# Adding the two states of a scan step on TensorE instead of GpSimd, with a refitted table of places

## The chip, the cores and the metric

The kernel runs on one core of one Trainium2 chip. The metric is the device time in microseconds of one launch. A core has five engines that work side by side and wait for each other by semaphores: TensorE (PE, with PEld for its weight loads), VectorE (DVE), ScalarE (ACT), GpSimd (POOL) and SyncE (SP), which here only issues DMAs. Everything is float32 except a few operands of the attention.

## What is computed

The input x (32 sequences of 256 positions with 256 channels) goes through four layers: a Mamba block on a permutation of the positions, softmax attention with 16 heads, a second Mamba block, and linear attention. The core of a Mamba block is a recurrence over the 256 positions for each of 512 channels and 16 states:

```python
def step(hst, inp):
    dt_t, B_t, C_t, x_t = inp
    dA = jnp.exp(dt_t[:, :, None] * A)
    hst = hst * dA + (dt_t * x_t)[:, :, None] * B_t[:, None, :]
    y = jnp.einsum('bds,bs->bd', hst, C_t)
    return (hst, y)
...
y = jnp.transpose(ys, (1, 0, 2)) + xm * D_param
y = y * jax.nn.silu(z)
return y @ W_out
```

The change is about the einsum: for every channel the 16 states, each multiplied by its row of C, are added up.

## The kernel before, in words

Two sequences are one group of T = 512 columns, and there are 16 groups. In each group each of the two Mamba blocks has one scan: the 512 channels are four chunks of 128 partitions, the 16 states are taken in pairs, and so a scan has 32 steps (STEPS, eight for each chunk, PER). There are 16 groups x 2 blocks x 32 = 1024 steps in all. A step handles two states of one chunk, side by side in a tile of 128 x 2 x 512:

- SyncE loads two rows of B into `bs` and two rows of C into `cs`, each spread over all partitions, 512 KB each (`scan_sync`, L1024). Each ring has two tiles. B's load of a step waits for the product (L952) two steps earlier, C's load for the multiplication by C (L984) two steps earlier, and both stand in one queue, in this order.
- ScalarE makes the decays `da` (L902), two instructions.
- VectorE multiplies dt*x, which lies in PSUM, by `bs` (L952) and runs the recurrence over the positions (L966), whose result is the tile `hw` of a ring of four (RING).
- GpSimd multiplies `hw` by `cs` (`times_c`, L984) and then adds the two halves of the tile (`add_pair`, L991).
- TensorE adds the 128 x 512 sum to the PSUM bank `yps` with a matmul by the identity (`reduce`, L853). The eight steps of a chunk accumulate there, started by the skip term (L868). Then VectorE multiplies the bank by silu(z) into `dtx` (`gated`, L935). The recurrence of a step may write its tile of the ring only when the matmul of four steps earlier is done.

Around the scans runs the rest of the network, the side work, on the same engines: the front of a Mamba block (layer norm, input projection, convolution of four taps on VectorE at L796, step sizes), its rest (z, the second half of the step sizes), its back (output projection L1056; in block 0 a gather of positions by one-hot matrices, L1066; gate and residual, L1094 and L1102), the attention of each sequence (scores and their maxima, L1207 and L1347; exponentials, L1313; product with V, L1251), and linear attention. While block 0 scans one group, block 1 scans the one before it, in turn, and the side work of neighbouring groups is laid among both.

Each engine has one queue. Its order is fixed by numbers: `PLACES` says for each piece of side work and each engine behind which part of which scan step an operation stands (5.442 is in step 5, behind 0.442 of it), and `AT` says where in a step the scan's own operations stand (the recurrence at 0.33, `reduce` at 0.3 with the tile of two steps earlier, the addition at 0.55). `iteration` merges the scan and two lanes of side work by these numbers. The middle groups run in a loop (`Fori`), the first and last ones are written out.

Of the kernel before, what the change touches and what calls it, by code (L numbers as in the profile page):

```python
# [192 lines left out]
AT = {"reduce": 0.3, "restart": 0.5, "decay": 0.1, "scan": 0.33, "times_c": 0.05, "add": 0.55, "load": 0.2, "chunk": 0.5}  # L193
# [10 lines left out]
        "pe": [-1.5, 0.8, 3.967, 6.633, 9.845, 10.391, 13.55],  # L204
        "act": [0.033, 0.067, 5.3, 5.9, 8.433, 9.433, 12.475, 12.6],
        "dve": [10.498, 10.832, 13.165, 14.11, 14.22],
        "pool": [11.3, 14.8, 15.3],
# [3 lines left out]
        "pe": [27.467, 27.633, 27.8, 27.967, 28.133, 28.55, 28.8, 29.05, 30.467, 30.633, 30.8, 31.133],  # L211
        "act": [24.35, 26.35, 26.6, 26.85, 28.211, 28.322, 28.433, 28.544, 28.656, 28.767, 28.878, 29.35, 29.6,
               29.85],
        "dve": [26.165, 26.247, 29.382, 29.433, 29.485, 29.536, 29.588, 29.639, 29.691, 29.742, 29.794, 29.845,
               29.897, 29.948, 30.553, 31.082, 31.165, 31.247],
        "pool": [26.8, 31.8, 32.05, 32.3],
# [3 lines left out]
        "pe": [24.8, 25.05, 25.54, 25.78, 26.02, 28.8, 30.55, 30.675, 30.8, 30.925, 31.175, 32.05],  # L220
        "act": [23.98, 24.6, 25.225, 25.35, 25.725, 25.85, 25.975, 29.331, 29.408, 29.485, 29.638, 29.792,
               29.869, 30.023],
        "dve": [23.665, 24.165, 26.665, 27.665, 28.11, 28.22, 28.665, 29.11, 29.22, 29.404, 29.553, 29.628,
               29.777, 29.926, 30.665, 31.497, 31.663, 31.83],
        "pool": [24.3, 31.8, 32.05, 32.3],
        "sp": [30.533, 30.867],
    },
    "back0": {
        "pe": [1.9, 3.467, 3.633, 3.8, 4.133],
        "act": [0.6, 4.433, 4.767, 5.5],  # L230
        "dve": [5.442, 5.553, 5.665, 5.777, 5.888],
        "pool": [-1.5, 2.3],
# [3 lines left out]
        "pe": [14.967, 17.7, 18.1],  # L236
        "act": [14.767, 20.9],
        "dve": [16.165, 16.665, 18.665, 19.165, 20.665],
        "pool": [20.717, 21.3],
# [7 lines left out]
        "act": [5.7, 6.6, 7.3, 8.211, 8.322, 8.544, 8.656, 8.767, 8.878, 8.989, 9.767, 11.433, 11.767, 12.225,  # L247
               12.35, 12.725, 12.85, 12.975, 14.433, 14.767, 15.3, 15.65, 15.725, 15.8, 15.875, 18.243, 18.386,
               18.529, 18.671, 18.814, 19.386, 19.529, 19.671, 19.814, 19.957, 20.3, 22.6, 23.7, 23.9],
        "dve": [6.11, 6.22, 8.665, 9.165, 10.414, 10.581, 10.665, 10.749, 10.916, 11.082, 11.165, 11.248,  # L250
               11.665, 16.553, 16.777, 17.165, 17.442, 17.553, 17.665, 17.777, 17.888, 18.165, 22.066, 22.132,
               22.198, 22.264, 24.665, 26.082],
        "pool": [6.8, 22.8, 24.217],
# [7 lines left out]
        "act": [0.025, 0.05, 0.075, 0.433, 0.767, 1.6, 3.267, 3.433, 3.6, 3.767, 8.267, 8.433, 8.6, 8.767,  # L261
               8.933, 9.211, 9.322, 9.433, 9.544, 9.656, 9.767, 9.989, 11.35, 11.6, 11.85, 15.3, 16.3, 16.5,
               16.7, 16.9, 17.267, 17.433, 17.6, 17.767, 17.933, 18.6, 20.3, 20.5, 20.7],
        "dve": [-1.5, -0.5, 2.665, 3.165, 4.665, 5.165, 5.665, 6.165, 6.665, 7.498, 7.665, 7.832, 8.165, 13.165,
               13.553, 13.777, 14.11, 14.22, 14.665, 15.11, 15.22, 15.553, 19.553, 19.777, 20.11, 20.22,
               22.553, 22.777],
        "pool": [0.275, 20.883, 21.8],
# [3 lines left out]
        "pe": [23.55, 24.05, 24.55, 26.26, 28.55, 29.05, 29.8, 30.425, 31.05, 31.55, 31.8],  # L271
        "act": [23.62, 23.74, 23.86, 25.475, 25.6, 26.433, 26.767, 29.177, 29.254, 29.562, 29.715, 29.946],
        "dve": [21.665, 22.165, 24.665, 25.165, 25.665, 26.11, 26.22, 26.497, 26.832, 27.165, 29.479, 29.702,
               29.851, 31.997, 32.163],
        "pool": [22.8, 30.217, 30.383],
# [3 lines left out]
        "pe": [17.05, 17.78, 18.729, 19.8, 20.133, 21.8, 22.467, 22.633, 25.7, 26.1, 30.967],  # L279
        "act": [15.575, 15.95, 16.025, 18.957, 19.243, 20.5, 20.7, 20.9, 21.6, 24.6, 24.85, 28.989],  # L280
        "dve": [15.165, 15.665, 18.665, 19.165, 19.497, 19.665, 19.832, 20.165, 20.665, 21.165, 23.165, 23.665,
               24.165, 28.665, 30.777],
        "pool": [16.3, 24.383, 27.8],
# [1569 lines left out]
```

## Time and profile before

| what | value |
|---|---|
| median of 3 runs | 5616.87 us |
| lowest and highest run | 5615.27 and 5630.38 us |
| profiled execution, its own time | 5616.71 us |
| span of its trace | 5614.9 us |
| VectorE busy | 4895.1 us (87%) |
| TensorE busy | 4463.3 us (79%) |
| GpSimd busy | 4077.3 us (73%) |
| ScalarE busy | 3463.0 us (62%) |

The span goes from the first to the last instruction of one execution. Busy is the time in which an engine had at least one instruction under way. A float32 matmul instruction appears as two records. Matmuls are pipelined, so the next one starts before the one ahead has ended, and a run of matmuls counts one such end as busy. PEclk is the granted TensorE clock as a share of the full one.

### The profile page before, as it was taken

How to read it: one execution, taken by the hardware profiler on the slowest of the kernel's cores; microseconds unless marked ns; L12 is line 12 of the kernel's file. 1: busy time of each engine (PE TensorE's matmuls, PEld its weight loads, DVE VectorE, ACT ScalarE, POOL GpSimd, SP SyncE). 2: the span in 40 equal slices, each digit the busy share in tenths (PEclk: the TensorE clock that was granted, in tenths of full speed). 3: DMA queues.
4: the chain of work that ended last, by engine and by line, in shares of the span. 5: the costliest groups of instructions: out<-in, count | busy, mean ns of one | idle time of the engine just before them, and what ended most of it. 6: DMA issues, size and time to landing. Idle time of an engine off the chain costs nothing.

```text
span 5614.9 us, 66460 instructions
## 1 busy us (share of the span) xinstructions
PE 4463.3 (79%) x15736; PEld 2300.2 (41%) x15736; DVE 4895.1 (87%) x5146; ACT 3463.0 (62%) x6182; POOL 4077.3 (73%) x2847
## 2 busy tenths in 40 slices
PE   4577888888788878888888888888788888888755
PEld 1233344444444434444444444444444444444323
DVE  3749999999999999999999999999999999999482
ACT  2346666667666666766666666766666676766352
POOL 2728787877878877777877777777877777787272
PEclk8678899999999999999999999999999899998775
DMA  4516666666667666666666666666666666666161
GB/s 143 193 64 232 213 231 214 225 219 207 233 202 228 225 219 221 212 229 201 224 225 221 218 219 224 207 227 212 222 212 223 219 210 228 214 228 209 63 209 51
DMA packets 350275, 1147.58 MB, mean 204 GB/s; under 512 B 38790, under 2 KB 79275, under 8 KB 349835
## 3 DMA queue, kind: packets, MB, share of 16 engines
q1 hardware_dynamic: 305674, 1088.05, 58.7%
q10 hardware_dynamic: 44160, 54.60, 3.1%
q8 instruction: 161, 2.64, 0.2%
q14 instruction: 280, 2.29, 0.1%
HBM read 1123.47 MB, written 19.04 MB: 203 GB/s over the span
## 4 chain that ended last, share of the span: by engine, by line
POOL 41%; issue 26%; DVE 12%; PE 10%; DMA 5%; ACT 4%; POOLq 1%; SPq 1%; DVEq 0%; ACTq 0%
POOL hw L984 30%; POOL hw L991 8%; DVE hw L966 5%; DMA cs<-bc_scratch 3%; DVE ps L952 3%; DMA bs<-bc_scratch 2%; PE ps L1139 1%; POOL rstd L611 1%; POOL dtx L840 1%; DVE u L796 1%; PE ps L853 1%; PE ps L677 1%; PE ps L1056 1%; PE ps L1148 1%; PE ps L1131 1%
## 5 line engine op out<-in xcount | busy, mean ns | idle before, releaser
L984 POOL TENSOR_TENSOR hw<-hw,cs 128x1024 f32<-128x1024 f32 x1024 | 2419.6, 2363 | 887.9 <-DVE hw L966 824.6
L966 DVE TENSOR_TENSOR_SCAN hw<-da,ps 128x1024 f32<-128x1024 f32 x1024 | 2334.2, 2279 | 59.7 <-ACT da L902 20.0
L902 ACT ACTIVATE da<-dt,a_neg 128x510 f32<-128x510 f32 x2048 | 1331.3, 714 | 359.9 <-DVE hw L966 357.8
L952 DVE TENSOR_TENSOR ps<-ps,bs 128x1024 f32<-128x1024 f32 x1024 | 1254.5, 1225 | 138.2 <-DMA bs<-bc_scratch 85.5
L991 POOL TENSOR_TENSOR hw<-hw 128x512 f32<-128x512 f32 x1024 | 1301.2, 1271 | 70.8
L853 PE MATMUL ps<-hw,ident 128*128 128x512 f32 x2048 | 1139.3, 663 | 129.1 <-POOL hw L991 128.8
L672 PE MATMUL ps<-hT,w_in 128*128 128x512 f32 x1024 | 532.6, 656 | 209.2 <-ACT sz L774 117.8
L853 PEld LDWEIGHTS ps<-hw,ident 128*128 128x128 f32 x2048 | 389.0, 208 | 571.3 <-issue 293.3
L1313 ACT ACTIVATE pts<-ps,mcur 128x256 f32<-128x256 f32 x1024 | 401.0, 476 | 251.6 <-PE ps L1236 249.8
L549 ACT ACT_TABLE_LOAD x353 | 452.9, 1283 | 54.7 <-issue 48.6
L1347 DVE TENSOR_REDUCE mx<-ps 128x2 f32<-128x512 f32 x512 | 330.0, 678 | 81.8 <-PE ps L1207 80.9
L672 PEld LDWEIGHTS ps<-hT,w_in 128*128 128x128 f32 x1024 | 190.2, 200 | 482.1 <-issue 231.4
L1200 PE MATMUL ps<-mb,pick 128*128 128x512 f32 x512 | 261.6, 547 | 127.5 <-DVE mx L1347 88.2
L1229 PE MATMUL ps<-nm,pick 128*128 128x512 f32 x512 | 243.7, 532 | 100.7 <-DVE nm L1352 66.2
L796 DVE SCALAR_TENSOR_TENSOR u<-ps,cols,u 128x510 f32<-128x510 f32 (+2 forms) x384 | 274.7, 735 | 34.2 <-ACT u L720 29.3
L1251 PE MATMUL ps<-pts,va 128*32 128x256 f32 x2048 | 276.2, 396 | 24.1 <-ACT pts L1313 22.5
L1056 PE MATMUL ps<-w_out,dtx 128*128 128x256 f32 x1024 | 249.2, 399 | 28.2 <-DVE dtx L935 26.5
L840 POOL TENSOR_TENSOR dtx<-dt,u 128x512 f32<-128x512 f32 x128 | 161.4, 1272 | 131.1 <-DVE dt L816 131.1
L1131 PE MATMUL ps<-rows,ones 1*128 1x512 f32 x320 | 188.9, 671 | 63.9 <-DVE xhat_b L1523 32.5
L1056 PEld LDWEIGHTS ps<-w_out,dtx 128*128 128x128 f32 x1024 | 199.9, 199 | 93.4 <-DVE dtx L935 34.5
L606 POOL TENSOR_TENSOR rstd<-mv,eps 128x2 f32<-128x2 f32 (+1 forms) x96 | 19.1, 199 | 279.6 <-DVE mv L601 277.8
L1200 PEld LDWEIGHTS ps<-mb,pick 128*128 128x128 f32 x512 | 96.0, 199 | 294.8 <-DVE mx L1347 206.6
(186 smaller groups left out, 5994.1 us busy)
## 6 DMA issues: line engine op xcount, KB each, us to landing
bs<-bc_scratch SPq DMA_DIRECT2D x1024, 512.0 KB, 5.0
cs<-bc_scratch SPq DMA_DIRECT2D x1024, 512.0 KB, 4.1
xhat<-in_x ACTq DMA_DIRECT2D x16, 512.0 KB, 4.4
gate<-gates_scratch ACTq DMA_DIRECT2D x64, 128.0 KB, 4.7
x_b<-in_x ACTq DMA_DIRECT2D x16, 512.0 KB, 7.3
x_scratch<-x_b ACTq DMA_DIRECT2D x16, 512.0 KB, 2.9
x_c<-x_scratch ACTq DMA_DIRECT2D x16, 512.0 KB, 5.5
out<-x_c ACTq DMA_DIRECT2D x32, 256.0 KB, 2.5
```

The costliest lines, as they stand in the source:

```text
L549: nc.scalar.preload_act_table_set(name)
L672: ins = nc.tensor.matmul(side[pc.bank[f"m{m}"]], w_in[l][:, k, m * P:(m + 1) * P], hT[:, k, :], start=(k == 0), stop=(k == DC - 1))
L796: nc.vector.scalar_tensor_tensor(out=um[:, :, s:], in0=bank[:, :, 0:S - s], scalar=col(f"m{l}_conv_w", m * TAPS + TAPS - 1 - s), in1=um[:, ...
L853: nc.tensor.matmul(yps, ident[:, :], hw[q % RING][:, 0, :], start=False, stop=(q % PER == PER - 1))\
L902: ins = nc.scalar.activation(da[q % (AHEAD + 1)][:, k, :, 1:S], dt_[:, c, :].rearrange("p (b s) -> p b s", b=GB)[:, :, 1:S], ACT.Exp, scal ...
L952: nc.vector.tensor_tensor(z, dxp.unsqueeze(1).broadcast_to([P, 2, T]), bs[s % B_RING][:, :, :], ALU.mult)\
L966: nc.vector.tensor_tensor_scan(tile[:, :, :].rearrange("p n t -> p (n t)"), da[s % (AHEAD + 1)][:, :, :, :].rearrange("p n b s -> p (n b s)"),
L984: nc.gpsimd.tensor_tensor(tile[:, :, :], tile[:, :, :], cs[s % C_RING][:, :, :], ALU.mult)\
L991: nc.gpsimd.tensor_tensor(tile[:, 0, :], tile[:, 0, :], tile[:, 1, :], ALU.add)\
L1056: ins = nc.tensor.matmul(side[pc.bank[key]][:, k * D:(k + 1) * D], dtx[l][:, c, r * P:(r + 1) * P], w_out[l][:, c, :], start=(c == 0), sto ...
L1200: nc.tensor.matmul(banks[hh].rearrange("p (h s) -> p h s", h=2), pick[:, 0:1].broadcast_to([P, P]), mb[:, :].unsqueeze(1).broadcast_to([P, ...
L1313: ins = nc.scalar.activation(pt[(2 * p + hh) % 4][:, t, :], side[pc.bank[f"t{p}{hh}"]][:, t * S:(t + 1) * S], ACT.Exp, bias=mcur[:, 1, t:t ...
```

## The change

`add_pair` and its place are taken out, so that GpSimd has one instruction for a step. `reduce` waits for the multiplication and issues two matmuls by the identity, one for each half of the tile, where it issued one. All of `PLACES` is replaced. Two of its twelve entries are shown in part.

```diff
-    pool = [f"{what}{q}" for q in range(STEPS) for what in ("mul", "add")]
+    pool = [f"mul{q}" for q in range(STEPS)]
...
-AT = {"reduce": 0.3, "restart": 0.5, "decay": 0.1, "scan": 0.33, "times_c": 0.05, "add": 0.55, "load": 0.2, "chunk": 0.5}
+AT = {"reduce": 0.3, "restart": 0.5, "decay": 0.1, "scan": 0.33, "times_c": 0.05, "load": 0.2, "chunk": 0.5}
...
     "back0": {
-        "pe": [1.9, 3.467, 3.633, 3.8, 4.133],
+        "pe": [2.2, 2.66, 2.82, 2.98, 3.14],
...
-        "dve": [5.442, 5.553, 5.665, 5.777, 5.888],
+        "dve": [5.041, 5.082, 5.124, 5.165, 5.206],
...
         def reduce(pe, l, g, q):
 
             pc = sc[l]
-            pe.wait_ge(pc.of(f"add{q}"), pc.upto(g, f"add{q}"))
-            nc.tensor.matmul(yps, ident[:, :], hw[q % RING][:, 0, :], start=False, stop=(q % PER == PER - 1))\
-              .then_inc(pc.next(f"red{q}"), 1)
+            pe.wait_ge(pc.of(f"mul{q}"), pc.upto(g, f"mul{q}"))
+            for k in range(2):
+                ins = nc.tensor.matmul(yps, ident[:, :], hw[q % RING][:, k, :], start=False,
+                                       stop=(k == 1 and q % PER == PER - 1))
+            ins.then_inc(pc.next(f"red{q}"), 1)
...
-        def add_pair(pool, l, g, s):
-
-            pc, tile = sc[l], hw[s % RING]
-            pool.wait_ge(pc.of(f"mul{s}"), pc.upto(g, f"mul{s}"))
-            nc.gpsimd.tensor_tensor(tile[:, 0, :], tile[:, 0, :], tile[:, 1, :], ALU.add)\
-              .then_inc(pc.next(f"add{s}"), 1)
-
         def scan_pool(pool, l, g, before, follows):
...
                 if s:
                     times_c(pool, l, g, s - 1)
-                    yield s + AT["add"]
-                    add_pair(pool, l, g, s - 1)
                 elif follows:
                     times_c(pool, 1 - l, before[1], STEPS - 1)
-                    yield s + AT["add"]
-                    add_pair(pool, 1 - l, before[1], STEPS - 1)
```

What the table moves is shown at one place, the start of block 1's scan in the loop, where the back of block 0 is done. Names are those of the program, with ring numbers; REGISTER_ALU and ISA rows are register and semaphore instructions. A sign ahead of a row says whether it is of the kernel before (-) or of the changed one (+). TensorE's queue before, from the output projection of the first sequence (L1056) on:

```order
-L1056 MATMUL ps<-w_out0,dtx0 128x256 x8
-L868 MATMUL ps<-u,diag_d 128x512
-L852 ISA
-L853 MATMUL ps<-hw0,ident 128x512
-L852 REGISTER_ALU
-L853 MATMUL ps<-hw1,ident 128x512
-L1056 MATMUL ps<-w_out0,dtx0 128x256 x8
-L1063 ISA
-L1066 MATMUL ps<-xhat,onehot 128x256 x4
-L1063 REGISTER_ALU
-L1066 MATMUL ps<-xhat,onehot 128x256 x4
```

The same of the changed kernel (L1044 is the output projection, L851 the matmul of `reduce`, L1054 the gather):

```order
+L1044 MATMUL ps<-w_out0,dtx0 128x256 x8
+L867 MATMUL ps<-u,diag_d 128x512
+L849 ISA
+L851 MATMUL ps<-hw0,ident 128x512 x2
+L1044 MATMUL ps<-w_out0,dtx0 128x256 x8
+L1051 ISA
+L1054 MATMUL ps<-xhat,onehot 128x256 x4
+L1051 REGISTER_ALU
+L1054 MATMUL ps<-xhat,onehot 128x256 x4
```

Between the two projections stand two matmuls by the identity in both: before for two steps (tiles hw0 and hw1), now for one (hw0, both halves), and the one for hw1 stands behind the gather.

VectorE's queue in the same stretch before, from the recurrence into hw0 to the first gate product (L1094), which reads what the gather left in PSUM:

```order
-L966 SCALAR_TENSOR_TENSOR hw0<-da1,ps 128x1024
-L948 REGISTER_ALU
-L952 TENSOR_TENSOR ps<-ps,bs1 128x1024
-L959 REGISTER_ALU
-L965 REGISTER_ALU
-L966 SCALAR_TENSOR_TENSOR hw1<-da2,ps 128x1024
-L510 REGISTER_ALU x3
-L1092 ISA
-L1093 ISA
-L1094 TENSOR_TENSOR ps<-ps,gate0 128x512
```

And of the changed kernel (L965 is the recurrence, L1082 the gate product):

```order
+L965 SCALAR_TENSOR_TENSOR hw0<-da1,ps 128x1024
+L947 REGISTER_ALU
+L951 TENSOR_TENSOR ps<-ps,bs1 128x1024
+L507 REGISTER_ALU x3
+L1080 ISA
+L1081 ISA
+L1082 TENSOR_TENSOR ps<-ps,gate0 128x512
```

The gate product now stands one recurrence earlier, ahead of the one into hw1.

## Rows read from the trace of the kernel before

**Rows 1.** The page, section 1: busy time, share of span, instructions.

```profile
PE 4463.3 (79%) x15736; PEld 2300.2 (41%) x15736; DVE 4895.1 (87%) x5146; ACT 3463.0 (62%) x6182; POOL 4077.3 (73%) x2847
```

**Rows 2.** Windows of 1000 us: PE, PEld, DVE, ACT, POOL busy (records), PEclk, DMA share, GB/s.

```profile
2000.00:3000.00 1000.00, 830.26 (x3021) 434.32 (x3022) 937.36 (x976) 666.49 (x1192) 783.43 (x540) 0.93 0.66 219
...
sum 4000.00, PE 3323.95 PEld 1728.22 DVE 3756.07 ACT 2664.45 POOL 3136.15; mean PE 830.99 PEld 432.06 DVE 939.02 ACT 666.11 POOL 784.04
```

**Rows 3.** The page, section 4: chain that ended last, by engine.

```profile
POOL 41%; issue 26%; DVE 12%; PE 10%; DMA 5%; ACT 4%; POOLq 1%; SPq 1%; DVEq 0%; ACTq 0%
```

**Rows 4.** The page, section 5: the scan's groups, busy, mean ns, idle before.

```profile
L984 POOL TENSOR_TENSOR hw<-hw,cs 128x1024 f32<-128x1024 f32 x1024 | 2419.6, 2363 | 887.9 <-DVE hw L966 824.6
L966 DVE TENSOR_TENSOR_SCAN hw<-da,ps 128x1024 f32<-128x1024 f32 x1024 | 2334.2, 2279 | 59.7 <-ACT da L902 20.0
L952 DVE TENSOR_TENSOR ps<-ps,bs 128x1024 f32<-128x1024 f32 x1024 | 1254.5, 1225 | 138.2 <-DMA bs<-bc_scratch 85.5
L991 POOL TENSOR_TENSOR hw<-hw 128x512 f32<-128x512 f32 x1024 | 1301.2, 1271 | 70.8
L853 PE MATMUL ps<-hw,ident 128*128 128x512 f32 x2048 | 1139.3, 663 | 129.1 <-POOL hw L991 128.8
```

**Rows 5.** Waits of VectorE between 1000 and 5000 us: total us, times, longest.

```profile
DVE ps L952 <- DMA bs<-bc_scratch: 63.1, 61, 3.1
DVE ps L952 <- ACT ps L916: 24.7, 32, 2.7
DVE stats L594 <- issue: 24.4, 11, 3.7
DVE nm L1352 <- ACT nm L1303: 21.9, 11, 2.6
DVE mx L1347 <- PE ps L1207: 18.9, 24, 2.0
DVE hw L966 <- ACT da L902: 17.1, 13, 1.4
DVE dt L810 <- PE ps L677: 9.3, 25, 1.0
DVE kT L1499 <- PE ps L1148: 7.9, 11, 1.0
DVE ps L1094 <- PE ps L1056: 6.7, 6, 2.2
DVE dt L816 <- ACT dt L762: 6.0, 17, 0.4
DVE x_b L1371 <- PE ps L1139: 2.1, 4, 0.9
DVE hw L966 <- PE ps L853: 1.4, 1, 1.4
```

**Rows 6.** Waits of POOL's multiplication over the whole span: total us, times, longest.

```profile
POOL hw L984 <- DVE hw L966: 824.6, 578, 8.8
```

**Rows 7.** Timeline of PE: start, length, matmul records by the identity.

```profile
2510.40 1.02 PE L853 MATMUL ps<-hw,ident 128*128 128x512 f32 x2
...
2518.57 1.88 PE L853 MATMUL ps<-hw,ident 128*128 128x512 f32 x4
```

**Rows 8.** Windows of 1000 us, line L853 alone, the sum.

```profile
sum 4000.00, PE 848.35 PEld 293.79; mean PE 212.09 PEld 73.45
```

**Rows 9.** Timeline, start of a scan of block 1: last gated product to first gate product.

```profile
2486.20 0.68 DVE L935 TENSOR_TENSOR dtx<-ps,sz 128x512 f32<-128x512 f32 x1
...
2490.65 1.23 DVE L952 TENSOR_TENSOR ps<-ps,bs 128x1024 f32<-128x1024 f32 x1 [1.57 <-DMA bs<-bc_scratch]
...
2494.48 1.23 DVE L952 TENSOR_TENSOR ps<-ps,bs 128x1024 f32<-128x1024 f32 x1 [0.28 <-DMA bs<-bc_scratch]
...
2498.19 1.23 DVE L952 TENSOR_TENSOR ps<-ps,bs 128x1024 f32<-128x1024 f32 x1 [0.16 <-DMA bs<-bc_scratch]
...
2501.66 0.67 DVE L1094 TENSOR_TENSOR ps<-ps,gate 128x512 f32<-128x512 f32 x1
```

**Rows 10.** The same stretch on PE: the gather.

```profile
2496.52 3.62 PE L1066 MATMUL ps<-xhat,onehot 128*128 128x256 f32 x16
```

More of the change, by code:

```diff
@@ L203 @@
     "rest1": {
[L204 to L207, printed above, removed]
+        "pe": [0.8, 1.6, 1.9, 5.633, 6.633, 7.586, 7.871],
+        "act": [0.3, 0.5, 0.7, 5.267, 5.933, 7.95, 8.025, 11.671],
+        "dve": [8.665, 9.03, 9.12, 11.11, 11.22],
+        "pool": [7.55, 11.55, 14.383],
         "sp": [-0.889, -0.778],
@@ L210 @@
     "front0": {
[L211 to L216, printed above, removed]
+        "pe": [27.633, 27.967, 28.383, 28.467, 28.55, 28.717, 28.8, 28.883, 29.05, 29.133, 29.217, 31.967],
+        "act": [23.95, 25.6, 26.433, 26.767, 28.2, 28.3, 28.5, 28.6, 28.8, 28.9, 29, 29.3, 29.5, 29.9],
+        "dve": [26.11, 26.22, 29.382, 29.433, 29.485, 29.536, 29.588, 29.639, 29.691, 29.742, 29.794, 29.845,
+               29.897, 29.948, 30.665, 31.132, 31.198, 31.264],
+        "pool": [26.55, 31.25, 31.45, 31.65],
         "sp": [30.533, 30.867],
@@ L219 @@
     "front1": {
[L220 to L226, printed above, removed]
+        "pe": [24.9, 25.1, 25.471, 25.643, 25.986, 26.157, 27.425, 27.55, 27.8, 27.925, 28.05, 32.05],
+        "act": [24.386, 24.529, 24.814, 24.957, 26.225, 26.35, 26.6, 26.725, 26.975, 28.267, 28.433, 28.6,
+               28.767, 29.85],
+        "dve": [23.904, 24.22, 26.464, 26.598, 26.732, 26.866, 27.082, 27.165, 27.247, 27.665, 28.066, 28.132,
+               28.198, 28.264, 29.082, 30.165, 31.165, 31.83],
+        "pool": [24.55, 30.55, 31.3, 31.8],
+        "sp": [29.533, 29.867],
     },
     "back0": {
-        "pe": [1.9, 3.467, 3.633, 3.8, 4.133],
-        "act": [0.6, 4.433, 4.767, 5.5],
-        "dve": [5.442, 5.553, 5.665, 5.777, 5.888],
-        "pool": [-1.5, 2.3],
+        "pe": [2.2, 2.66, 2.82, 2.98, 3.14],
+        "act": [0.9, 2.6, 3.433, 3.767],
+        "dve": [5.041, 5.082, 5.124, 5.165, 5.206],
+        "pool": [1.55, 2.55],
         "sp": [-0.444, -0.333],
@@ L235 @@
     "back1": {
[L236 to L239, printed above, removed]
+        "pe": [13.8, 14.8, 14.967],
+        "act": [13.433, 18.85],
+        "dve": [15.832, 16.11, 16.665, 17.066, 17.198],
+        "pool": [12.8, 18.383],
         "sp": [-0.667, -0.556],
@@ L242 @@
     "attn_a": {
[4 rows of a table removed]
[L247 to L253, printed above, removed]
[3 rows of a table added]
+        "act": [5.433, 5.6, 5.767, 7.233, 7.367, 7.575, 7.65, 7.725, 7.8, 7.875, 9.35, 9.6, 9.85, 10.433,
+               10.767, 11.243, 11.386, 11.529, 11.814, 11.957, 13.243, 13.386, 13.529, 13.671, 13.957, 15.95,
+               16.433, 16.767, 18.211, 18.322, 18.433, 18.544, 18.989, 19.35, 19.6, 19.85, 22.6, 23.65, 23.8],
+        "dve": [5.248, 5.289, 7.553, 7.777, 9.06, 9.09, 9.15, 9.18, 9.21, 9.24, 9.27, 9.3, 9.665, 15.553,
+               15.777, 16.082, 16.165, 16.247, 16.497, 16.665, 16.832, 17.165, 22.066, 22.132, 22.198, 22.264,
+               24.665, 25.165],
+        "pool": [5.55, 22.383, 22.717],
         "sp": [-0.222, -0.111],
@@ L256 @@
     "attn_b": {
[4 rows of a table removed]
[L261 to L267, printed above, removed]
[3 rows of a table added]
+        "act": [0.025, 0.05, 0.075, 1.767, 2.5, 2.7, 4.243, 4.386, 4.529, 4.671, 7.9, 8.211, 8.322, 8.433,
+               8.544, 8.878, 8.989, 9.6, 11.433, 11.767, 12.6, 13.267, 13.6, 13.767, 13.933, 16.35, 16.6,
+               16.85, 18.35, 18.6, 19.35, 19.6, 19.85, 20.243, 20.386, 20.814, 22.3, 22.7, 24.243],
+        "dve": [-1.5, -0.5, 2.665, 3.665, 6.442, 6.553, 6.665, 6.777, 7.11, 7.22, 7.498, 7.832, 8.165, 14.665,
+               15.165, 15.498, 15.665, 16.055, 16.165, 16.22, 16.275, 17.132, 21.464, 21.598, 21.732, 21.866,
+               23.617, 23.809],
+        "pool": [0.525, 21.55, 23.55],
         "sp": [-0.222, -0.111],
@@ L270 @@
     "lin_a": {
[L271 to L275, printed above, removed]
+        "pe": [19.8, 20.133, 20.633, 24.5, 25.814, 26.329, 27.675, 28.175, 29.8, 31.55, 31.8],
+        "act": [20.529, 20.671, 20.957, 22.5, 22.9, 23.8, 24.671, 26.475, 26.85, 28.933, 29.35, 29.6],
+        "dve": [17.264, 17.665, 22.11, 22.22, 22.665, 23.165, 23.426, 23.521, 23.713, 24.11, 28.665, 29.165,
+               29.247, 31.58, 32.08],
+        "pool": [18.717, 29.55, 31.55],
         "sp": [-0.444, -0.333],
@@ L278 @@
     "lin_b": {
[L279 to L283, printed above, removed]
+        "pe": [14.8, 16.8, 18.02, 19.9, 20.8, 21.633, 22.633, 25.9, 28.633, 28.967, 31.633],
+        "act": [13.814, 15.65, 15.8, 18.656, 18.767, 18.878, 21.6, 22.35, 22.85, 28.4, 28.7, 29.7],
+        "dve": [13.665, 14.165, 17.665, 18.665, 19.165, 19.553, 19.777, 20.165, 20.665, 21.165, 24.165, 27.665,
+               29.165, 30.165, 31.066],
+        "pool": [14.717, 29.55, 31.85],
         "sp": [-0.667, -0.556],
@@ L1596, in iteration @@
                     times_c(eng, 1 - seg, near["before"][1], STEPS - 1)
-                    add_pair(eng, 1 - seg, near["before"][1], STEPS - 1)
                 elif follows and e == "dve":
```

8 lines of the change are left out of this document (4 added, 4 removed), and 14 rows, old and new, of the table PLACES.

## The prediction

> **What bounds the kernel now.** I read the busy times first. VectorE is busy 87% of the span, TensorE 79%, GpSimd 73% [rows 1]. Those are averages over a filling, a steady middle and a draining part, so I then read the middle: between 1000 and 5000 us VectorE is busy 3756 of 4000 us, 94%, TensorE 3324 (83%) and GpSimd 3136 (78%) [rows 2]. VectorE is the bound there, and the change gives it no work and takes none away. So the change can only act on the 4000 - 3756 = 244 us in which VectorE stands still, and on the ramps.
>
> The chain that ended last gives another picture: 41% of it is GpSimd and 12% VectorE [rows 3]. The reader should see how both can be true. B's load stands in SyncE's queue behind C's load, and C's load waits for GpSimd's multiplication, so a chain traced back from VectorE's wait for `bs` soon arrives on GpSimd. It says that GpSimd is near the bound, not that its work is what VectorE waits for. That is in VectorE's waits [rows 5]: 63 us on the load of `bs`, 25 on the copy of dt*x, 24 at the loop's turn ("issue"), and 46 us on TensorE directly (18.9 + 9.3 + 7.9 + 6.7 + 2.1 + 1.4).
>
> **Removed from GpSimd.** 1024 additions of 1271 ns, 1301 us of busy time [rows 4]; GpSimd falls to 4077 - 1301 = 2776 us, 49%. Only what VectorE waited for is time. The multiplication stood waiting for the recurrence in 578 of 1024 steps [rows 6]; in the other 446 it began late, and only there can the removal bring a `cs` load, and the `bs` load behind it, forward. The floor of the gain is 0, if transfers are slow by themselves; the ceiling is all 85.5 us that VectorE waited for `bs` in the span [rows 4]. I take the share of late steps: 85.5 x 446/1024 = **37 us gained**.
>
> **Added to TensorE.** 1024 matmul instructions. A pair of records alone takes 1.02 us and two pairs in a row 1.88 us [rows 7], so one more behind another costs 0.86 us, and 1024 cost 881 us. By busy time TensorE goes to 4463 + 881 = 5344 us, 95% of the span. In the middle, line L853 had 848 us [rows 8]; its records there are the same share of 4000 us as 790 steps, whose second matmuls cost 790 x 0.86 = 679 us, and 3324 + 679 = 4003 of 4000. That is no proof that it doesn't fit, because busy counts ends that overlap once matmuls are denser: L853's 848 us over 790 calls are 1.07 us each where 0.86 would do, a ratio of 0.80. If that held for all lines, TensorE needs 0.80 x 3324 + 679 = 3340 us, 83%. So TensorE lies between 83% and full, beside a VectorE of 94%, and each hands work to the other.
>
> What hides the second matmul now is TensorE's idle time, 676 us of the 4000. Where that cover is gone, everything queued behind a `reduce` comes 0.86 us later: scores for the maxima, projections for convolution and step sizes, the back's products. VectorE's direct waits on TensorE are 46 us, and two of its waits on ScalarE are one TensorE result further on (`nm` 21.9, `dt` 6.0), 74 us together [rows 5]. The floor of the increase is 0, if the refitted table lays all of it under cover. For my value I let these waits grow as TensorE's idle time halves, that is double: 74 more in 4000 us, and with the middle's rate over the whole span (x 5615/4000 = 1.4, less in the solo scans at both ends, so I use 1.2) **+89 us**. The ceiling is that TensorE becomes the bound, below.
>
> TensorE's wait is shorter too: it waited for the addition and now for the multiplication, 1.27 us sooner, and then works 0.86 us longer. `reduce` ends 0.4 us earlier where TensorE is free. VectorE's recurrence waited for it 1.4 us in the middle [rows 5], so this is worth nothing.
>
> **Moved by the table.** Every operation is still there once, on its engine, so a place costs only what VectorE comes to wait. I followed one chain. From the end of the gated product (2486.88) TensorE runs projection, skip term, two matmuls by the identity, projection, gather; the gather starts at 2496.52 and half of it, enough for the first sequence, is done near 2498.4: 11.5 us [rows 9, 10]. The changed queue holds the same matmuls in this stretch. VectorE came to the gate product after 14.8 us, of which 2.0 us were waits for `bs`. Now there is one recurrence less before it: 14.8 - 2.0 - 2.3 = 10.5 us, so it would wait 1.0 us if no `bs` wait remains and 0 if they remain. Over 15 groups 0 to 15 us, and similar gains may exist elsewhere. With both signs open I put 0 for the table and keep VectorE's other idle time as the bound for a gain.
>
> **The sum.** 5616.7 (the profiled execution: span 5614.9 and 1.8 around it; the median of the runs is 0.2 higher) - 37 + 89 + 0 = 5668.7, and I say **5668 us**, 0.9% slower. This forecast's own range is 5635 (only a fifth more wait) to 5740.
>
> **Rivals.**
>
> *GpSimd's lateness was the real limit (faster).* For it: 41% of the chain, and late steps in 446 of 1024. Mechanism: with one instruction a step GpSimd is always in time, the loads of `cs` and `bs` go out as soon as the recurrence allows, all 85.5 us vanish, and the 24.7 us on the copy of dt*x, which comes behind GpSimd's dt*x product, vanish also. TensorE's queue stays in time. 5616.7 - 85.5 - 25 x 1.2 = 5501 at most; half of it is likelier, 5559 us. It decides if TensorE's new waits stay under some 50 us. Against it: 61 waits for 63 us in the middle are 1 us each and the transfer has its own length.
>
> *The denser TensorE keeps its clock (faster).* The granted clock is 0.93 to 0.94 of full in the middle [rows 2]. As the levels are 1.2 and 2.4 GHz, some 12 to 14% of that time passes at the lower one, at double cost for each matmul. If added matmuls fill the idle stretches that precede the lower level, the clock goes towards 1.0, and 0.065 x 3324 = 216 us of TensorE's time comes back in the 4000, a third of what is added. Then its waits don't grow and the 37 us stay: 5580 us. The Trainium skill ("TensorE: Matmul & The Clock Gate", "Why this matters for your kernels") advises to avoid idle gaps between bursts of matmuls so that the clock stays up; by that rule the sum would come to this 5580, and by the row alone, with the clock as it was, to 5668. The rows of before don't tell how far 0.94 can rise.
>
> *TensorE becomes the bound (much slower).* If the 4003 us by busy time are near the truth, its necessary waits for its own suppliers come on top. It idled 676 of 4000 us; if a quarter of that can't be filled, 169 us or 4.2% is added in the middle: 5616.7 + 0.043 x 4700 = 5819 us. The recurrence would show it, waiting for `reduce` four steps back, and so would the maxima.
>
> *Nothing comes of it.* The gain of 37 and a growth of waits by half (45) cancel: 5620 us. That the change doesn't do what it says is hardly possible: the queues show one GpSimd row and two matmuls a step.
>
> **Chances.** Forecast 0.38; TensorE as the bound 0.13; cancelling 0.17; GpSimd's lateness 0.18; the clock 0.14. A measurement of this kernel tells about 0.3% (17 us) from no change. So faster 0.32, same 0.17, slower 0.51. The range for 8 in 10 leaves out the lower end of the GpSimd rival and the upper half of the TensorE one: 5530 to 5800 us.
>
> **What would show it.** GpSimd's busy time near 2776 us with 1024 rows fewer; L851 with 4096 records and some 2000 us; TensorE's busy time 5200 to 5350; VectorE's 4895 unchanged. For the forecast: VectorE's waits on TensorE in the middle at 80 to 120 us in place of 46, its waits for `bs` at 30 to 45 in place of 63, PEclk 0.94 to 0.97. For the GpSimd rival: the multiplication waits for the recurrence in nearly all steps and `bs` is under 15 us. For the clock: 0.98 or more, and waits on TensorE at or below 46. For TensorE as the bound: the recurrence waiting on L851 for more than 50 us. The forecast is wrong if VectorE's busy share in the middle stays at 94% or rises, since nothing else can keep the time or shorten it.

## The result and the profile after

The changed kernel takes **5783.49 us** (median of 4 runs, 5768.45 to 5804.9) against 5623.62 us of the kernel before in 4 runs beside it: ratio **1.029**, 95% interval 1.0261 to 1.032. That is 163 us by the ratio, where the sum had 52. The profiled execution took 5786.49 us, 1.8 us of it around its span. The changed kernel is slower, as forecast; the size is three times the forecast's, and 5783 lies above the forecast's own range (5635 to 5740), inside the wide one.

The page after, section 1, with the start of section 4 and five groups of section 5 (columns as in [rows 4]); they answer to [rows 1, 3, 4]:

```profile
PE 5061.4 (87%) x17784; PEld 2626.0 (45%) x17784; DVE 4938.2 (85%) x5146; ACT 3443.2 (60%) x6168; POOL 2796.0 (48%) x1823
...
DVE 24%; issue 24%; PE 16%; DMA 16%; POOL 13%; ACT 4%; SPq 1%; DVEq 1%; POOLq 0%; ACTq 0%
...
L983 POOL TENSOR_TENSOR hw<-hw,cs 128x1024 f32<-128x1024 f32 x1024 | 2420.6, 2365 | 2067.6 <-DVE hw L965 1998.3
L965 DVE TENSOR_TENSOR_SCAN hw<-da,ps 128x1024 f32<-128x1024 f32 x1024 | 2335.5, 2281 | 48.7 <-PE ps L851 15.2
L851 PE MATMUL ps<-hw,ident 128*128 128x512 f32 x4096 | 1975.3, 615 | 41.9 <-POOL hw L983 41.6
...
L951 DVE TENSOR_TENSOR ps<-ps,bs 128x1024 f32<-128x1024 f32 x1024 | 1256.9, 1227 | 183.2 <-DMA bs<-bc_scratch 156.0
...
L1335 DVE TENSOR_REDUCE mx<-ps 128x2 f32<-128x512 f32 x512 | 332.1, 682 | 116.3 <-PE ps L1195 116.3
```

GpSimd is relieved as computed (1024 instructions fewer, 2796 us), and it now waits 1998 us for the recurrence where it waited 825. Yet VectorE's wait for `bs`, the very one that the relief was to shorten, **grew from 85.5 to 156.0 us**. VectorE's busy time grew by 43 us with the same 5146 instructions and the same mean durations to 2 ns in the scan's two groups; that was not in the prediction at all.

The middle, windows of 1000 us (columns of [rows 2]), one of them and the sum:

```profile
2000.00:3000.00 1000.00, 916.11 (x3300) 480.36 (x3301) 915.78 (x944) 638.93 (x1148) 519.24 (x332) 0.97 0.66 211
...
sum 4000.00, PE 3669.03 PEld 1920.38 DVE 3680.90 ACT 2566.79 POOL 2088.57; mean PE 917.26 PEld 480.10 DVE 920.23 ACT 641.70 POOL 522.14
```

VectorE's share fell from 94% to 92%, TensorE's rose to 92%, and its granted clock from 0.93 to 0.97. VectorE's waits there (total us, times, longest), which answer to [rows 5]:

```profile
DVE ps L951 <- DMA bs<-bc_scratch: 121.2, 136, 3.7
DVE mx L1335 <- PE ps L1195: 42.2, 80, 1.5
DVE stats L591 <- issue: 28.0, 11, 3.1
DVE ps L1082 <- PE ps L1044: 24.9, 12, 2.7
DVE dt L813 <- ACT dt L759: 14.5, 24, 0.8
DVE qhl L1326 <- ACT qhl L1272: 10.6, 12, 0.9
...
DVE dt L807 <- PE ps L674: 7.6, 23, 0.5
DVE qsm L1495 <- PE ps L1127: 6.8, 12, 3.0
DVE hw L965 <- PE ps L851: 6.5, 18, 0.9
DVE nm L1340 <- ACT nm L1291: 2.6, 4, 0.8
```

The recurrence hardly waits for TensorE (6.5 us), so TensorE did not become the bound. The maxima and the gate product wait more (the gate's 12 waits all stand in block 1's back, none in the back of block 0); `nm` and the copy of dt*x, which waited 22 and 25 us, wait 3 and almost nothing. The largest item is the load of B.

### The profile page after: what moved, and what is told of

Its sections match the earlier page's. It is cut to its first block, busy times and chain, and to the rows that moved or that the text cites. A ratio compares the mean times of both kernels' runs of the same rounds, so it can differ in the third digit from the quotient of the medians.

```text
span 5784.7 us, 68750 instructions
## 1 busy us (share of the span) xinstructions
PE 5061.4 (87%) x17784; PEld 2626.0 (45%) x17784; DVE 4938.2 (85%) x5146; ACT 3443.2 (60%) x6168; POOL 2796.0 (48%) x1823
## 4 chain that ended last, share of the span: by engine, by line
DVE 24%; issue 24%; PE 16%; DMA 16%; POOL 13%; ACT 4%; SPq 1%; DVEq 1%; POOLq 0%; ACTq 0%
DMA bs<-bc_scratch 12%; POOL hw L983 11%; DVE hw L965 11%; DVE ps L951 5%; DMA cs<-bc_scratch 4%; PE ps L851 3%; PE ps L1127 2%; PE ps L1044 2%; DVE mx L1335 2%; PE ps L1119 1%; ACT da L901 1%; PE ps L1136 1%; PE ps L1188 1%; DVE u L793 1%; DVE stats L591 1%
## 5 line engine op out<-in xcount | busy, mean ns | idle before, releaser
L965 DVE TENSOR_TENSOR_SCAN hw<-da,ps 128x1024 f32<-128x1024 f32 x1024 | 2335.5, 2281 | 48.7 <-PE ps L851 15.2
L851 PE MATMUL ps<-hw,ident 128*128 128x512 f32 x4096 | 1975.3, 615 | 41.9 <-POOL hw L983 41.6
L951 DVE TENSOR_TENSOR ps<-ps,bs 128x1024 f32<-128x1024 f32 x1024 | 1256.9, 1227 | 183.2 <-DMA bs<-bc_scratch 156.0
L851 PEld LDWEIGHTS ps<-hw,ident 128*128 128x128 f32 x4096 | 759.1, 195 | 851.7 <-issue 715.5
L669 PE MATMUL ps<-hT,w_in 128*128 128x512 f32 x1024 | 488.8, 611 | 31.9 <-ACT sz L771 18.6
L1188 PE MATMUL ps<-mb,pick 128*128 128x512 f32 x512 | 271.7, 576 | 118.6 <-DVE mx L1335 112.6
L1044 PE MATMUL ps<-w_out,dtx 128*128 128x256 f32 x1024 | 263.6, 416 | 25.9 <-DVE dtx L934 24.2
L1044 PEld LDWEIGHTS ps<-w_out,dtx 128*128 128x128 f32 x1024 | 210.3, 210 | 84.5 <-DVE dtx L934 29.3
L1291 ACT ACTIVATE nm<-ps 8x256 fp32r<-8x256 f32 x64 | 23.9, 373 | 375.7 <-PE ps L1203 375.7
L1239 PE MATMUL ps<-pts,va 128*32 128x256 f32 x2048 | 238.3, 390 | 2.7 <-ACT pts L1301 2.7
```

The lines of the kernel that those rows point to most:

```text
L669: ins = nc.tensor.matmul(side[pc.bank[f"m{m}"]], w_in[l][:, k, m * P:(m + 1) * P], hT[:, k, :], start=(k == 0), stop=(k == DC - 1))
L851: ins = nc.tensor.matmul(yps, ident[:, :], hw[q % RING][:, k, :], start=False, stop=(k == 1 and q % PER == PER - 1))
L951: nc.vector.tensor_tensor(z, dxp.unsqueeze(1).broadcast_to([P, 2, T]), bs[s % B_RING][:, :, :], ALU.mult)\
L965: nc.vector.tensor_tensor_scan(tile[:, :, :].rearrange("p n t -> p (n t)"), da[s % (AHEAD + 1)][:, :, :, :].rearrange("p n b s -> p (n b s)"),
L1044: ins = nc.tensor.matmul(side[pc.bank[key]][:, k * D:(k + 1) * D], dtx[l][:, c, r * P:(r + 1) * P], w_out[l][:, c, :], start=(c == 0), sto ...
L1188: nc.tensor.matmul(banks[hh].rearrange("p (h s) -> p h s", h=2), pick[:, 0:1].broadcast_to([P, P]), mb[:, :].unsqueeze(1).broadcast_to([P, ...
```

## Why a relieved GpSimd does not bring B sooner

SyncE's queue holds, in this order, B's load of step s, C's of step s, B's of step s+1. C's load of step s waits for the multiplication of step s-2. So B's load of step s+1, whose own tile is free as soon as the product of step s-1 is done, is held until that multiplication is done. What SyncE's queue waits for between 1000 and 5000 us, in the kernel before and then in the changed one:

```profile
SPq L1024 <- POOL hw L984: 2954.7, 790, 8.9
...
SPq L1024 <- DVE ps L952: 91.0, 79, 3.4
```

```profile
SPq L1012 <- POOL hw L983: 3052.3, 766, 13.5
SPq L1012 <- DVE ps L951: 108.2, 82, 2.6
```

The page after, section 6, load of B (KB, median us from issue to landing):

```profile
bs<-bc_scratch SPq DMA_DIRECT2D x1024, 512.0 KB, 5.0
```

The queue stands on GpSimd in both kernels. Now take a run of steps with no side work between them, in which VectorE's product and recurrence take 1.23 and 2.29 us, about 3.6 us a step with the gaps. GpSimd in time starts the multiplication when the recurrence ends and needs 2.37 us; B's load is issued 0.43 us behind C's (2785.16 and 2785.59 in the timeline below) and takes 5.0 us to land (the page's DMA issues, median): 7.8 us. VectorE wants it after two steps, 7.2 us. **Even a GpSimd that is never late delivers B 0.6 us late there.** Only side work between the steps hides it. The refitted table leaves more such bare steps: counted in the timeline, about 17 steps in a loop pass of 64 are shorter than 3.9 us where 12 were. In the middle, 107 of 767 products could have started less than 7.9 us after the end of the recurrence three steps back, and 78 of the 121 us of waits for B are theirs; before the change it was 9 of 790 products and 4 of 63 us. The multiplication was over 0.15 us late in 300 of 936 steps of the loop before and in 75 now, and the waits for B doubled all the same.

The longest single item is at step 47 of the pass (step 15 of its second scan), 3.18 us on average. The timeline of the changed kernel (start, length), VectorE, then SyncE's queue, then ScalarE's:

```profile
2787.55 2.29 DVE L965 TENSOR_TENSOR_SCAN hw<-da,ps 128x1024 f32<-128x1024 f32 x1
2789.75 0.67 DVE L1335 TENSOR_REDUCE mx<-ps 128x2 f32<-128x512 f32 x1
2793.69 1.23 DVE L951 TENSOR_TENSOR ps<-ps,bs 128x1024 f32<-128x1024 f32 x1 [3.27 <-DMA bs<-bc_scratch]
...
2785.16 0.32 SPq L1012 DMA_DIRECT2D cs<-bc_scratch  x1
2785.59 0.37 SPq L1012 DMA_DIRECT2D bs<-bc_scratch  x1
...
2784.76 0.34 ACTq L565 DMA_DIRECT2D x_c<-x_scratch  x1
```

The load of B issued at 2785.59 is there 8 us later instead of 5. A load of 512 KB for `x_c` was issued 0.8 us before it on another queue, and two loads of 128 KB (`gate`) on that queue 1.4 and 1.9 us before it.

## The experiments

Each kernel ran on one chip with runs of the kernel before, and its ratio is to those. "The second matmul" is the one that the change adds to a step.

| kernel | table | GpSimd adds | matmuls a step | B's load | median us | ratio (95%) | clock |
|---|---|---|---|---|---|---|---|
| before | old | yes | 1 | behind C | 5624 to 5633 | 1 | 0.90 |
| after | new | no | 2 | behind C | 5783.5 | 1.029 (1.0261 to 1.032) | 0.94 |
| e1 | old | no | 2 | behind C | 5861.4 | 1.0405 (1.0366 to 1.0443) | 0.94 |
| e2 | new | yes | 1 | behind C | 5945.9 | 1.0561 (1.0515 to 1.0607) | 0.87 |
| e3 | new | no | 1 | behind C | 5850.5 | 1.0398 (1.0359 to 1.0436) | 0.88 |
| e4 | old | yes | 2 | behind C | 5857.4 | 1.0401 (1.0359 to 1.0442) | 0.94 |
| e5 | new | no | 2 | first | 5629.5 | 1.0006 (0.9991 to 1.0022) | 0.96 |
| e6 | old | yes | 1 | first | 5547.7 | 0.9859 (0.983 to 0.9887) | 0.90 |
| e7 | new | no | 2 | behind C | 5762.1 | 1.0249 (1.0221 to 1.0277) | 0.95 |
| e8 | old | yes | 1 + 128 columns | behind C | 5622.6 | 0.9991 (0.9978 to 1.0004) | 0.91 |
| e9 | old | yes | 1 + 256 columns | behind C | 5683.9 | 1.009 (1.0059 to 1.0121) | 0.92 |
| e10 | old | no | 2 | first | 5780.7 | 1.0261 (1.0227 to 1.0294) | 0.95 |
| e11 | new | no | 1 | first | 5732.2 | 1.0181 (1.0146 to 1.0216) | 0.89 |
| e12 | new | no | 1 + 128 columns | behind C | 5840.1 | 1.0365 (1.033 to 1.04) | 0.90 |

(e7 also shortens the load of `x_c`. The clock is the mean over the profiled span. Differences between kernels of this table are of their medians, if nothing else is said; where two kernels were timed beside different runs of the kernel before, the ratios give up to 13 us more or less.)

### Each part of the change alone: e1 to e4

e1 is the changed kernel with the table of before:

```diff
 PLACES = {
     "rest0": {
-        "pe": [-1.5, 3.033, 3.633, 4.633, 4.967, 8.55, 8.8],
+        "pe": [-1.5, 0.633, 3.967, 4.967, 5.633, 9.845, 11.8],
...
```

> TensorE adds both halves, but with the table of places of the kernel before. If the refitted table is what costs the time, this stays near the kernel before, 5590 to 5650 us. If the doubled matmuls cost it, a table fitted to single matmuls can only be worse: 5780 us or more.

e2 is the kernel before with the refitted table:

```diff
 PLACES = {
     "rest0": {
-        "pe": [-1.5, 0.633, 3.967, 4.967, 5.633, 9.845, 11.8],
+        "pe": [-1.5, 3.033, 3.633, 4.633, 4.967, 8.55, 8.8],
...
```

> GpSimd multiplies and adds and TensorE has one matmul a step, as before, but with the refitted table. If the table costs the time: 5740 to 5830 us. If the doubled matmuls cost it: 5610 to 5660 us.

e3 takes the second matmul out of the changed kernel:

```diff
-            for k in range(2):
+            for k in range(1):
                 ins = nc.tensor.matmul(yps, ident[:, :], hw[q % RING][:, k, :], start=False,
-                                       stop=(k == 1 and q % PER == PER - 1))
+                                       stop=(q % PER == PER - 1))
```

> The changed kernel without the second matmul of a step, so the second state of every pair is left out of the sum: TensorE's load is that of before, GpSimd's that of the change. If the table costs the time, 5740 to 5790 us; if TensorE's load does, 5620 to 5660 us.

e4 adds a second matmul to the kernel before and leaves GpSimd's addition in:

```diff
-            nc.tensor.matmul(yps, ident[:, :], hw[q % RING][:, 0, :], start=False, stop=(q % PER == PER - 1))\
-              .then_inc(pc.next(f"red{q}"), 1)
+            for k in range(2):
+                ins = nc.tensor.matmul(yps, ident[:, :], hw[q % RING][:, 0, :], start=False,
+                                       stop=(k == 1 and q % PER == PER - 1))
+            ins.then_inc(pc.next(f"red{q}"), 1)
```

> The kernel before with its addition on GpSimd and its table, and with the matmul of every step issued twice on the same half (the sum is counted twice): TensorE's load of the change alone. If the load costs the time, 5750 us or more; if the table does, 5620 to 5650 us. The difference to the kernel with the same table and no addition is what relieving GpSimd gives: 0 to 40 us.

Measured, with the old table: the second matmul costs 230 us (5627.1 of before in this group to e4's 5857.4), and taking the addition from GpSimd then changes nothing (e1, 5861.4). The refit brings back 1.15 points of ratio, some 65 us (e1 to after; 78 by the medians). With the new table everything is worse without the matmul than with it: 5945.9 with GpSimd adding, 95 us less without the addition (e3), and **67 us less again when the second matmul is added** (after; 61 by the ratios). e2 and e3 came out slower than either of their two expectations, so the new table is dear beside one matmul in a way that none of them held. So the parts don't add up one by one: the table costs 319 us in the kernel before and saves 65 beside two matmuls.

e1's waits of VectorE between 1000 and 5000 us show where the 230 us are:

```profile
DVE ps L954 <- ACT ps L918: 70.7, 56, 2.9
DVE ps L954 <- DMA bs<-bc_scratch: 52.6, 46, 3.6
DVE mx L1338 <- PE ps L1198: 48.3, 55, 1.6
DVE nm L1343 <- ACT nm L1294: 44.1, 35, 4.3
DVE dt L810 <- PE ps L677: 39.8, 36, 1.8
DVE hw L968 <- ACT da L904: 35.2, 37, 1.5
```

These are TensorE's results at second hand: the copy of dt*x, the decays and `nm` by ScalarE, and `dt` and `mx` directly. They are the waits that the refit removed (copy 70.7 to nearly 0, `nm` 44.1 to 2.6, `dt` 39.8 to 7.6), and it paid with those for B (52.6 to 121.2). The waits for B, of e4 and then of e2, tell which part moves them:

```profile
DVE ps L954 <- DMA bs<-bc_scratch: 51.0, 41, 3.3
```

```profile
DVE ps L949 <- DMA bs<-bc_scratch: 124.3, 131, 3.4
```

With the old table they are 63.1 us before, 51.0 with the second matmul (e4) and 52.6 with GpSimd relieved as well (e1). With the new one they are 124.3 with GpSimd still adding (e2), 95.5 with it relieved (e3) and 121.2 with the second matmul too. **So the table doubles them; the relief of GpSimd leaves them as they were or shortens them.**

### B's load ahead of C's: e5, e6, e10, e11

The edit issues B's load of the next step ahead of C's load of this one, and nothing else:

```diff
                 yield s - B_RING + 1 + AT["load"]
-                slice_in(bs[s % B_RING], s, B_RING, 0, "dbx", b_in)
+                for q in ([0, 1] if s == 0 else [s + 1] if s + 1 < STEPS else []):
+                    slice_in(bs[q % B_RING], q, B_RING, 0, "dbx", b_in)
                 slice_in(cs[s % C_RING], s, C_RING, NS, "mul", c_in)
```

e5 is the changed kernel with it:

> The changed kernel with one thing moved: SyncE issues B's load of the next step ahead of C's load of this one, so that B's load waits only for the product two steps earlier and no longer behind a wait for GpSimd. If VectorE's 121 us of waits for bs in the middle come from that queue, they fall below 50 us and the time to 5650 to 5710 us. If the transfers themselves are too slow where steps stand bare, the waits stay over 90 us and the time at 5760 to 5800 us.

e6 is the kernel before with it:

> The same move in the kernel before. If the queue holds B's loads back: waits for bs in the middle fall from 63 to under 30 us and the time to 5560 to 5600 us. If the transfers bound them: 5610 to 5640 us.

e5's waits of SyncE's queue, then of VectorE, 1000 to 5000 us:

```profile
SPq L1012 <- DVE ps L951: 2357.5, 749, 8.6
SPq L1012 <- POOL hw L983: 816.5, 644, 9.1
```

```profile
DVE ps L951 <- DMA bs<-bc_scratch: 26.6, 27, 3.3
DVE mx L1336 <- PE ps L1196: 26.3, 63, 0.8
...
DVE ps L1083 <- PE ps L1045: 11.9, 7, 1.9
DVE qhl L1327 <- ACT qhl L1273: 10.5, 12, 0.9
```

The queue now stands on VectorE's product, which is B's own condition, and the wait for B falls from 121.2 to 26.6 us (in e6 from 63.1 to 5.5). The changed kernel gains 154 us (5783.5 to 5629.5; 160 by the ratios), the kernel before 83 (5631.2 to 5547.7). 82 us stay between the two (5629.5 against 5547.7, timed together). **So about 80 of the 163 us are the order of the two loads, which this change made dearer without touching it.** The gain in e5 is more than the wait for B: VectorE's direct waits on TensorE fell with it, from 96.0 to 64.8 us, and both kernels came out faster than the ranges expected. e6 is also the fastest kernel of the study, 1.4% under the kernel before.

e10 is e1 with the edit, e11 is e3 with it:

> TensorE adds both halves, table of before, B's loads ahead of C's. If the 230 us of this table are all TensorE's load, the loads give about what they gave the kernel before (83 us): 5770 to 5790 us. If part of the 230 are loads held back: under 5740 us.

> The refitted table, B's loads ahead, and one matmul a step (the second state of a pair is left out). With C's loads ahead this one matmul less made the kernel 67 us slower (5850 to 5783) at a clock of 0.88 to 0.94. If the clock does this, it stays slower than with both matmuls: 5670 to 5720 against 5630. If the loads did it: 5600 to 5630.

e10 gained 81 us (5861.4 to 5780.7), e11 118. With B out of the way the refit is worth 151 us beside two matmuls (e10 to e5), more than twice the 65. And e11, with half the accumulation left out, is **103 us slower than e5, which has it** (99 by the ratios). That speaks for the clock, which is lower in e11 (0.89 against 0.96 over the span). The line of two of TensorE's groups, those that differ most, in e11 and then in e5, 1000 to 5000 us (busy, mean ns):

```profile
L1128 PE MATMUL ps<-w_l_v,hT_b 128*128 128x256 f32 x192 | 72.0, 540 | 0.0
L1137 PE MATMUL ps<-hT_a,w_a_q 128*128 128x256 f32 x192 | 70.1, 529 | 13.3 <-ACT hT_a L1266 13.3
```

```profile
L1137 PE MATMUL ps<-hT_a,w_a_q 128*128 128x256 f32 x200 | 50.4, 396 | 14.4 <-ACT hT_a L1266 14.4
...
L1128 PE MATMUL ps<-w_l_v,hT_b 128*128 128x256 f32 x192 | 47.9, 392 | 0.0
```

The same matmuls take 529 and 540 ns in the one and 396 and 392 in the other. Most groups differ less (the output projection 421 against 401 ns, the matmul of `reduce` 645 against 604). What waits for TensorE waits longer; e11's waits of VectorE:

```profile
DVE mx L1336 <- PE ps L1196: 36.7, 69, 1.0
DVE qhl L1327 <- ACT qhl L1273: 30.0, 12, 3.0
...
DVE ps L951 <- DMA bs<-bc_scratch: 26.7, 32, 3.5
DVE ps L1083 <- PE ps L1045: 23.6, 12, 2.7
```

`qhl`, behind the q-projection (L1137), waits 30.0 us against 10.5; the gate 23.6 against 11.9; `mx` 36.7 against 26.3. B is equal, 26.7 and 26.6. All direct waits on TensorE are 118.6 us against 64.8.

### How the cost of added matmuls grows: e8, e9, e12

e8 adds a matmul of 128 columns to the kernel before, e9 one of 256:

```diff
-            nc.tensor.matmul(yps, ident[:, :], hw[q % RING][:, 0, :], start=False, stop=(q % PER == PER - 1))\
-              .then_inc(pc.next(f"red{q}"), 1)
+            ins = nc.tensor.matmul(yps, ident[:, :], hw[q % RING][:, 0, :], start=False, stop=False)
+            ins = nc.tensor.matmul(yps[:, 0:128], ident[:, :], hw[q % RING][:, 0, 0:128], start=False,
+                                   stop=(q % PER == PER - 1))
+            ins.then_inc(pc.next(f"red{q}"), 1)
```

e9 is the same with 256 in place of 128.

> The kernel before with a further matmul of 128 columns behind the one of every step, a quarter of the added work of the change (128 columns are counted twice). If TensorE's added work costs in proportion (230 us for 512 columns with this table): 5627 + 58 = 5685 us. If the cost starts only where TensorE has no idle time left, or if a denser TensorE gets its clock up and that pays: 5600 to 5640 us.

> The kernel before with a further matmul of 256 columns a step, half of the change's added work (256 columns counted twice). 128 columns cost nothing (5623), 512 cost 230 us. If cost starts where TensorE's idle time is used up: 5660 to 5720 us, well under half of 230 above 5631. If it is a step caused by the further instruction's length in one place: either 5630 or 5850.

With the old table 128, 256 and 512 columns (e8, e9, e4) cost -9 (within the interval of no change), +51 and +230 us: nothing at first, then steeply. e9's waits on ScalarE's copy (38.1 us) and on `da` (29.4) lie between those of before and of e1, in the same places. So the cost does not go by the length. That it begins where no idle time is left ahead of results that are due fits these waits, but no run shows it apart from them.

e12 is the same with the new table: only 128 of the second matmul's 512 columns.

```diff
+            nc.tensor.matmul(yps, ident[:, :], hw[q % RING][:, 0, :], start=False, stop=False)
+            ins = nc.tensor.matmul(yps[:, 0:128], ident[:, :], hw[q % RING][:, 1, 0:128], start=False,
+                                   stop=(q % PER == PER - 1))
```

> The refitted table and a second matmul of only 128 of 512 columns (the rest of the second state is left out). If a denser TensorE keeps its clock up, the clock lies between 0.88 and 0.94 and the time between 5783 and 5850, near 5810. If the second matmul helps by its place alone, or not by the clock, the time has no such relation: 5850 or 5783 at an unchanged clock of 0.88.

It came to 5840.1 at a clock of 0.90: 10 us less than without them (5850.5 at 0.88), with 512 columns at 5783.5 and 0.94. Clock and time go together, but the 10 us are within both intervals. e12 does not decide; the reading rests on e3 against after and e11 against e5.

### The load beside B's: e7

```diff
-                act.dma_start(x_c[:, :, :], x_dram).then_inc(xc_in, 16)
+                w = D if first else 32
+                act.dma_start(x_c[:, :, 0:w], x_dram[:, :, 0:w]).then_inc(xc_in, 16)
```

> The changed kernel in which the residual load of block 1's back (x_c from x_scratch, 512 KB) brings 32 of 256 channels after the first group; the rest of the residual is left out. The table put this load next to step 15 of block 1's neighbour scan, where VectorE waits 3.2 us for bs in every loop pass. If the two transfers collide, that wait goes and the time falls by 35 to 60 us, to about 5735. If the queue behind GpSimd makes it, the time stays within 10 us of 5783.

The stall at step 47 fell from 3.18 to 1.4 us, VectorE's wait for B in the middle from 121.2 to 98.1, and the time by 21 us to 5762.1, between the two expectations (the ratio intervals overlap from 1.0261 to 1.0277, so the 21 us are at the edge of what can be told). So `x_c` makes a little more than half of that one stall. What makes the rest was not taken apart: B's late issue gives 0.6 us by the sum above, and the two `gate` loads still stood ahead.

### VectorE's own stream is longer with the new table

VectorE's busy time over all runs splits by the table alone. The page's section 1 of e1 and of e6 (old table), then of e2 and of e11 (new table):

```profile
PE 5094.9 (87%) x17784; PEld 2648.4 (45%) x17784; DVE 4910.0 (84%) x5146; ACT 3462.7 (59%) x6182; POOL 2794.1 (48%) x1823
```

```profile
PE 4438.9 (80%) x15736; PEld 2294.2 (41%) x15736; DVE 4893.8 (88%) x5146; ACT 3463.0 (62%) x6182; POOL 4071.7 (73%) x2847
```

```profile
PE 4582.9 (77%) x15736; PEld 2385.2 (40%) x15736; DVE 4942.7 (83%) x5146; ACT 3441.7 (58%) x6168; POOL 4069.6 (68%) x2847
```

```profile
PE 4502.8 (79%) x15736; PEld 2344.5 (41%) x15736; DVE 4934.5 (86%) x5146; ACT 3442.7 (60%) x6168; POOL 2792.9 (49%) x1823
```

Seven kernels with the old table have 4894 to 4911 us, seven with the new one 4933 to 4943, whatever TensorE, GpSimd and the loads do. The timeline of VectorE before shows what differs:

```profile
2603.04 2.29 DVE L966 TENSOR_TENSOR_SCAN hw<-da,ps 128x1024 f32<-128x1024 f32 x1
2605.36 1.23 DVE L952 TENSOR_TENSOR ps<-ps,bs 128x1024 f32<-128x1024 f32 x1
2606.50 0.68 DVE L935 TENSOR_TENSOR dtx<-ps,sz 128x512 f32<-128x512 f32 x1
2607.10 1.39 DVE L594 BATCH_NORM_STATS2 stats<-xhat 128x6 f32<-128x256 f32 x4
```

The product starts 0.03 us after the recurrence has ended (2605.33). The gated product starts 0.09 us *before* the product has ended (2606.59), the statistics 0.08 us before the gated product has. I summed these gaps between 1000 and 5000 us, leaving out those of 0.3 us and more, which are waits. Product to recurrence and recurrence to product: +0.04 us each. A scan operation beside a side operation: -0.06 to -0.08. Before, there were 591 neighbours of the first kind and 1978 of the second; after, 731 and 1607, because the new table lays side operations one behind the other and leaves steps bare. All gaps together are -136.2 us before and -93.0 after: **43 us of overlap lost in the middle** (53 over the whole span), beside 60.7 us more of waits (198.1 to 258.8). A loop pass of 64 steps went from 324.2 to 334.6 us; of these 10.4, waits are 5.6, lost overlap 3.3, and longer durations 0.8.

## Why the prediction was wrong in its size

- **What bounds.** Right: the middle sets the time, and VectorE's own stream and waits account for nearly all of it (9.7 of 10.4 us a pass). TensorE at 92% did not become the bound; the recurrence waited 6.5 us for `reduce`.
- **The wait for B: 37 us gained by the relief, 0 by the table.** This is the step that failed. `bs` waits rose from 85.5 to 156.0 us in the span, 70 us worse where the sum had 37 better, and that is nearly all of the 111 us by which the sum was short. The table raised them, in the middle from 63.1 to 124.3 us with GpSimd's work unchanged (e2); the sum had put the table at nothing after following one chain, in which it counted the waits for B without asking what sets them. The prediction names the queue in which B stands behind C, and then does not work out its time: 7.8 us against two bare steps of 7.2. The 37 us themselves, priced by the share of late multiplications (which did fall to a quarter), were mis-sized either way: the relief is worth 0 with the old table (e4 to e1) and 95 with the new (e2 to e3). Also, the 446 steps without a wait for the recurrence were not all late; counted at 0.15 us, 322 of 1024 were.
- **Added to TensorE: 89 us.** VectorE's direct waits on TensorE were 96 us where 80 to 120 stood as the mark, twice the 46 as said; those by way of ScalarE (`nm`, `dt`, now `qhl`) stayed at 28. That is 50 more in the middle instead of 74, or 60 instead of 89 over the span. It holds only with the refit: by itself the matmul costs 230 (e4), so the method of doubling was near for a reason it did not have.
- **The table: 0.** The chain that was followed was read rightly: the gate product of block 0's back, forecast at 0 to 1.0 us a group, does not wait at all in the middle. But another gate product, that of block 1's back, waits 24.9 us in 12 loop passes (6.7 before), and the places changed what they were not read for: more bare steps, thus B's waits and 43 us of overlap. "VectorE's 4895 unchanged" was 4938. By itself the table costs 319 us (e2), and beside two matmuls it saves 65.
- **Lines up to the 163.** Between the two traces lie 170 us. VectorE's gaps of 0.3 us and more grew by 104 (the wait for B by 70, TensorE's direct waits by about 60, while the copy of dt*x, 24.7 us in the middle, vanished), its overlap shrank by 53, and its instructions took 12 us longer. This says where the time lies; what caused it is told by the runs of parts above, and they do not add up.
- **Rivals.** GpSimd as the limit: its multiplication waits for the recurrence in 940 of 1024 steps, as that rival wanted, and the 85.5 us did not vanish. TensorE as the bound: not seen; that its 5819 is nearer to the measured time than the 5668 is luck. (Two sums of rivals are 5 us off: 5616.7 - 37 + 45 is 5625, and 4.2% of 4700 us gives 5814.) The clock: the granted clock rose from 0.93 to 0.97, below the 0.98 of that rival, and the waits on TensorE doubled, so it did not decide. In the kernel before, the granted clock varies from run to run: in the 19 runs beside e5 and e6 it lies between 0.894 and 0.904, and the time is lower by about 23 us for each 0.01 more (a fit of mine; in e5's ten runs 38 us; in the four runs each of e10 and e12 there is no such relation). Which of the two leads is not shown. But the rival's mechanism is likely there, since the second matmul makes the kernel 67 and 103 us *faster* where the places are the new ones. The Trainium skill ("TensorE: Matmul & The Clock Gate", "Why this matters for your kernels") advises to avoid idle gaps between bursts of matmuls; the clock in e5 against e11 (0.99 against 0.92 in the middle) agrees with it. With the old table the clock rises too (0.90 to 0.94, e4) and the kernel is 230 us slower, so the rule says nothing of the price.
- **Open.** That the clock is the whole of the 67 and 103 us is argued from equal queues, longer matmuls and longer waits behind them. No edit changed the clock with the same matmuls. That the refit's 151 us shrinks to 65 with B behind C fits the bare steps. Why the table costs 319 us beside one matmul is open: B's waits and the overlap are a part of it, and direct waits on TensorE at 161.1 us (e2) against 47.4 another. The overlap alone was not varied either.
